# Two transformer layers on one core: VectorE takes the rectified feed-forward banks itself

## What is computed

```
h = concatenate([x, -x])
h = s0 * (h @ (+-1 matrix, 256 x 512));  h = relu(h) * 2
h = s1 * (h @ (+-1 matrix, 512 x 512));  h = relu(h) * 2
h = s2 * (h @ (+-1 matrix, 512 x 128))
x = x + attention(xn) + h
```

## Time and profile before

| | us |
|---|---|
| median of the runs | 918.23 |
| the profiled execution, its own time | 919.21 |
| its span, first to last instruction | 916.9 |
| PE busy | 849.4 |
| ACT busy | 774.9 |
| DVE busy | 528.3 |

### The profile page before, as it was taken

How to read it: one execution, slowest core, us unless ns; L and a number is a source line. 1 busy time by engine, 2 the same in 40 slices (tenths; PEclk the granted TensorE clock), 3 DMA queues, 4 the chain that set the end, 5 groups by cost and what they waited for, 6 DMA issues and landing times. The chain is left out here.

```text
span 916.9 us, 18621 instructions
## 1 busy us (share of the span) xinstructions
PE 849.4 (93%) x7071; PEld 321.8 (35%) x7071; DVE 528.3 (58%) x1273; ACT 774.9 (85%) x866; POOL 25.0 (3%) x39
## 2 busy tenths in 40 slices
PE   9568887999999999999999999999999789999996
PEld 7122222343333323333333333333343223333342
DVE  7076468575774666745765556745776266366321
ACT  1568997788889998999888998899988599889884
POOL 1000000000000000000000000000000000000000
PEclk9779999899999999999999999999999799999998
DMA  3855506513527216360427306270336404107000
GB/s 89 177 101 125 66 3 187 122 22 49 166 53 146 27 47 154 96 97 1 140 60 147 45 2 198 66 126 2 111 89 130 61 1 142 50 1 195 5 13 12
DMA packets 43893, 76.13 MB, mean 83 GB/s; under 512 B 6496, under 2 KB 8416, under 8 KB 43792
## 3 DMA queue, kind: packets, MB, share of 16 engines
q1 hardware_dynamic: 42492, 71.53, 35.3%
q10 hardware_dynamic: 668, 1.25, 0.7%
q0 software_dynamic: 640, 2.10, 0.7%
HBM read 37.37 MB, written 35.65 MB: 80 GB/s over the span
## 5 line engine op out<-in xcount | busy, mean ns | idle before, releaser
L662 ACT ACTIVATE probs<-ps_s 128x1024 f32<-128x1024 f32 x768 | 732.7, 1037 | 94.4 <-PE ps_s L817 91.3
L836 PE MATMUL ps_pv<-probs,v_aug 128*32 128x512 f32 x3072 | 415.1, 613 | 7.6 <-ACT probs L662 3.8
L817 PE MATMUL ps_s<-q_ab,k_ab 18*128 18x512 f32 (+1 forms) x1088 | 143.9, 501 | 29.4 <-ACT probs L662 17.4
L817 PEld LDWEIGHTS ps_s<-q_ab,k_ab 18*128 18x128 f32 (+1 forms) x1088 | 54.9, 185 | 170.7 <-ACT probs L662 121.9
L836 PEld LDWEIGHTS ps_pv<-probs,v_aug 128*32 128x32 f32 x3072 | 61.6, 108 | 118.0 <-issue 79.6
L687 PE MATMUL ps_misc<-h_hi,k_w 128*128 128x512 f32 x192 | 86.1, 448 | 2.7 <-ACT ff_out L627 1.2
L817 PE MATMUL ps_s<-q_c,k_c 34*128 34x512 f32 x448 | 82.3, 445 | 0.0
L1239 DVE COPY pv_sb<-ps_pv 128x512 f32<-128x512 f32 x48 | 33.2, 691 | 75.3 <-PE ps_pv L836 72.6
L688 PE MATMUL ps_misc<-h_lo,k_w 128*128 128x512 f32 x192 | 76.3, 397 | 0.0
L1057 DVE CAST h_hi<-ff_out 128x512 fp32r<-128x512 f32 x64 | 27.4, 427 | 79.5 <-ACT ff_out L627 77.7
L687 PEld LDWEIGHTS ps_misc<-h_hi,k_w 128*128 128x128 f32 x192 | 36.1, 188 | 87.2 <-issue 41.1
(11 more groups left out here) (142 smaller groups left out, 593.8 us busy)
## 6 DMA issues: line engine op xcount, KB each, us to landing
parts_dram<-qk_parts SPq DMA_DIRECT2D x32, 512.0 KB, 3.7
parts_dram<-qk_parts SPq DMA_DIRECT2D x62, 256.0 KB, 4.0
q_ab<-parts_dram SPq DMA_DIRECT2D x64, 128.0 KB, 4.5
k_ab<-parts_dram SPq DMA_DIRECT2D x60, 128.0 KB, 5.9
q_c<-parts_dram SPq DMA_DIRECT2D x14, 512.0 KB, 7.7
k_c<-parts_dram SPq DMA_DIRECT2D x14, 512.0 KB, 8.0
x_all<-in_L_attn_x_dram SPq DMA_DIRECT2D x8, 256.0 KB, 8.8
out_dram<-x_all POOLq DMA_DIRECT2D x8, 256.0 KB, 6.6
```

The costliest lines, as they stand in the source:

```text
L662: nc.scalar.activation(probs[:, U.slot(s), 2 * half:2 * half + 2], ps_s[:, 2 * pair:2 * pair + 2], ACT.Exp, scale=SCALE[U.layer]).then_inc ...
L817: ins = nc.tensor.matmul(ps_s[:, bank, :], k[row:row + n, slot, c * P:(c + 1) * P], q[row:row + n, slot, :], start=True, stop=True)
L836: ins = nc.tensor.matmul(ps_pv[32 * j:32 * j + 32, :], v_aug[:, U.v, c, a:a + 32], probs[:, U.slot(s), j, :], start=c == 0 and not odd, st ...
```

## The change

The 64 banks of `ff0` and `ff1_b` are now counted as taken by DVE. The Relu instruction of ACT and its two waits are gone. DVE waits for the job itself, reads the bank twice (once for the high part with `max(x, 0)`, once for the low part with `max(x, 0) - hi`), waits for its own second instruction, and then raises `job_taken`, which frees the bank. `ff2_b` stays with ACT.

```diff
-             project0="dve", project1="dve", ff0="act", ff1="act", ff1_b="act", ff2="act", ff2_b="act", ff_t="dve")
+             project0="dve", project1="dve", ff0="dve", ff1="dve", ff1_b="dve", ff2="act", ff2_b="act", ff_t="dve")
...
-                elif name in ("ff0", "ff1_b"):
-
-                    wait(act, ff_split, 2 * (2 * NF * b + (0 if name == "ff0" else NF) + item[2]))
-                    nc.scalar.activation(ff_out[:], ps_misc[:], ACT.Relu).then_inc(job_taken_act, 1)
...
-                wait_taken(dve, (name, b, f))
-                settled()
-                nc.vector.tensor_copy(hi, ff_out[:]).then_inc(ff_split, 1)
+                dve.wait_ge(job_made, PLAN.made[name, b, f])
+                settled()
+                nc.vector.tensor_scalar(hi, ps_misc[:], 0.0, None, ALU.max).then_inc(ff_split, 1)
                 dve.wait_ge(ff_split, n + 1)
-                nc.vector.tensor_tensor(lo, ff_out[:], hi.bitcast(F32), ALU.subtract).then_inc(ff_split, 1)
+                nc.vector.scalar_tensor_tensor(lo, ps_misc[:], 0.0, hi.bitcast(F32), ALU.max, ALU.subtract).then_inc(ff_split, 1)
+                dve.wait_ge(ff_split, n + 2)
+                dve.sem_inc(job_taken, 1)
                 last[:] = ff_split, n + 2
```

## The result

The changed kernel takes 947.9 us (median of 4 runs, 946.7 to 953.3); the kernel before, 917.8 (4 runs). The ratio is 1.033, with a 95% interval from 1.028 to 1.038: slower by 30 us. The forecast was 945 us, range 931 to 955.

A forecast was written before the change was run, and what follows sets the result against it. PE, 93% busy, bounds the kernel and waits for banks held too long: 16.0 (loop) + 2.2 + 2.8 + 4.8 + 0.9 - 0.4 + 0.7 = 27.0 us on 919.2, 946.2; less 1.0 to the median, 945 us, range 931 to 955.

The forecast's parts named there:

- head of LAST: Same places as the loop, but DVE free at `ff0` 3 and `k0` a step later: 2.2 us lost.
- `ff0` 0 of sequence 6: Split stands behind both halves of `rope` q while `k1` wants the bank: 2.8 us lost, the largest single term.
- six more places: Banks in sequences 0, 6 and 7 where DVE is late, each 0.4 to 1.2, taken at 0.8: 4.8 us lost.
- the step with two `ff0`: DVE, busy with layer norm, holds both banks; PE's wait for ACT goes, but it waits for layer norm: 0.7 us lost.
- tail of LAST: Four places with DVE free lose 0.9 us; one with 0.62 of ACT's lateness gives back 0.4.
- The hold: Bank held 1.59 us from the job's end, wanted after 1.36: 0.23 us too long even with DVE idle.
- rival 2: High part runs at 0.43 us from PSUM, so a smaller loss: 13 us less, 932 us; chance 0.09.
- rival 1: ACT is what pays and no bank wait appears: 4.5 us faster, 914 us; chance 0.05.
- rival 4: DVE's slack takes the waits in as PE and DVE settle in another rhythm: 918 us; chance 0.04.
- the 0.48 us: PE's wait ahead of its values after two neighbouring `ff0`, put down to a late exponential on ACT: 5 x 0.48 = 2.4 us.
- ACT busy near 736: Sign in the profile after: ACT's busy time in us, with 39.1 us of Relus removed.
- rival 3: PE's clock falls after longer waits, 5 us on top: 950 us, or 956 with both reads at 0.75; chance 0.12.

The follow-up runs named there:

- Experiment 3: Changed kernel, but DVE first copies the bank out with max(x, 0) into `ff_out`, then makes both parts from there; 932.7 us, ratio 1.015 to the kernel before.
- experiment 1: Changed kernel with only the `ff1_b` banks taken by DVE, those of `ff0` through ACT's Relu as before; 929.7 us, ratio 1.012 to the kernel before.
- experiment 2: Changed kernel with only the `ff0` banks taken by DVE, those of `ff1_b` through ACT's Relu as before; 939.4 us, ratio 1.020 to the kernel before.
- Experiment 5: Kernel before, with only `ff0` 0 of sequences 1 to 5 taken by DVE straight from the bank; 917.4 us, one run.
- experiment 4: Changed kernel with DVE's split put ahead of its other work at five kinds of place, PE's order untouched; 942.6 us, ratio 1.027 to the kernel before.
- experiment 7: Changed kernel with DVE's split put ahead of its other work, except `ff0` 3 ahead of `rope` k; 943.3 us, ratio 1.027 to the kernel before.

## Why the prediction was right

Own steps of the prediction against step lengths, profiled execution after minus before:

| place | predicted | measured |
|---|---|---|
| `ff0` 0 and 1 with ACT's 0.48 (loop) | 0.0 | +0.2 - 0.2 |
| `ff0` 2 before `out_t1` | 0.87 | 0.94 |
| `ff0` 3 before `v1` | 1.21 | 1.29 |
| `ff1_b` 0 and 1 | 0.46 | 0.40 |
| `ff1_b` 2 before `regroup` | 0.69 | 0.64 |
| `ff1_b` 3 before `k0` | 0.79 | 0.90 |
| one sequence in the loop | 4.0 | 4.2 |
| head of LAST | 2.2 | 2.2 |
| `ff0` 0 of sequence 6 | 2.8 | 2.9 |
| six more places | 4.8 | 4.9 |
| the step with two `ff0`, and three on | 0.7 | 0.2 |
| tail of LAST | 0.5 | 0.6 |
| every other step, start and end | 0 | -0.3 |
| whole span | 27.0 | 27.2 |

In the row of every other step, one near 580 is 0.95 us longer, where PE stands 0.78 us without a releaser in the profile; the steps ahead of sequence 1 are 0.6 shorter. That these cancel, and so the closeness of 27.2 to 27.0, is luck; the agreement of the single places is not.

- **The hold** was the right quantity. `q0`'s pair priced it at 1.59 us; it is 1.57. The high part from PSUM takes 0.69 us. Experiment 3, which shortens the hold and lengthens the work, confirms it against DVE's load. A TENSOR_SCALAR of the same size from SBUF takes 426 ns (L988), like the conversion, so it is the source that costs, and rival 2 is out. The rule of the Trainium skill, page "VectorE: DVE Perf Modes", section "Why PSUM operands drop a tier", that float32 from PSUM gets the single rate, holds here (691 ns); the double rate that the same page's tier table allows from PSUM did not appear.
- **The places** add up, as experiments 1 and 2 show step by step.
- **Rivals 1 and 4** are out: ACT only waits more (163.0 us against 91.3), and the span grew by the waits.
- **Wrong in its mechanism: the 0.48 us.** I took the profile's "<- ACT" at its word, where the wait also counts `take`. The number came out, because both go with the Relu of `ff0` 0: that is luck.
- **Wrong: "ACT busy near 736".** It fell by 27 us, to 748, not by 39. I subtracted the Relus' 39.1 us whole, but in the trace of the kernel before their spans overlap those of the exponentials beside them, by 11.6 us in all (one at 462.67 lasts until 463.27, and the next exponential starts at 463.17); that time was busy anyway.
- **Mis-sized: the step with two `ff0`.** The waits are near the 1.5 and 2.3 us that rival 3 names (1.42 and 2.56 us), but 0.2 us was lost and not 0.7. In the kernel before, `q0` of sequence 2 fell into the low clock from 160.1 to 166.9; in the kernel after, the low clock came from 157.6 to 164.4, and `q0`'s step is 1.87 us shorter. Experiment 5 shows that this is the clock: with the same two waits as in the kernel before (1.20 and 1.58 us) and no low clock there, that step has the same 2.29 us. So the term came out small by where the clock fell, and not by anything that the prediction worked out; rival 3 had put an earlier low stretch down as a loss.
- **Rival 3** is real and smaller than priced. In the profiled execution after, the clock held through the 2.66 us wait before `k1`. In experiments 2, 3, 4 and 7 it fell behind or within shorter ones (1.1 to 1.9 us). The four runs of the changed kernel took 946.7, 948.2, 947.6 and 953.3 us at mean granted clocks of 0.978, 0.978, 0.976 and 0.971. The median's growth of 30 us, against 27 for the profiled executions, may be that, or the spread between executions; it was not tested.

## What to carry to other kernels

When two stages share one bank, price a change of the reader by how long it holds the bank against how long the writer can do without it (here 1.36 us, one step of other work), and only then by how busy the reader is: copying out first with the idle engine cost 0.6 us of hold, two direct reads 1.57. Where the reader's queue has other work ahead, add the end of that work. And a wait that moves to the engine which sets the pace can cost again through its clock, so a sum of waits can come out short (experiments 2 to 4 and 7), or, where a low stretch moves off a busy step, long.

## Of the hardware, not expected

- PE's granted clock went down to 0.5 behind or within single waits of 1.1 to 1.9 us in kernels whose PE is busy for over 90% of the span (experiments 2, 3, 4, 7; in 2 and 7 a second wait of 0.81 us followed), yet not behind one of 2.66 us in the profiled execution after. It also fell at 125.1 us in experiment 1, within a 1.16 us wait for `take`; the kernel before has the same wait (up to 126.65) without a fall. The mean clock differs between executions of a kernel: experiment 4 had 0.961 to 0.971, and 949.6 to 939.0 us.
- TENSOR_SCALAR with max and SCALAR_TENSOR_TENSOR with max and subtract, from a PSUM bank to float32r, took 691 ns each, no more than the one-operation copies of the same shape from PSUM (L1251, L1121: 0.69 us): the second operation and the rounding added nothing that the rows show.
- Behind the second read, the wait for it and the increment cost 0.1 us until PE's next job (476.50 to 476.62), in experiment 3's direct increment 0.06 us (479.20 to 479.26).
